# Three-layer decoder on one core: the mask of two pairs added by VectorE, with the setup and the order of work rearranged

## The reference, cut to what matters

```
layer 0: causal self-attention, 16 heads, then x @ W_proj
layer 1: q from x; k, v from ctx; scores = where(mask == 0, -1e9, q k^T / 4); softmax; @ wo
layer 2: unmasked self-attention + mixture of 8 experts (softmax gate, top 2, x @ W_experts[e] + b)
x = layernorm(x + layer(x))
```

## Time and profile before

| | |
|---|---|
| median of 3 runs | 925.97 us (924.67 to 928.93) |
| profiled execution, its own time | 927.58 us |
| its span | 925.8 us |
| mean granted TensorE clock | 0.991 of full speed |
| PE / VectorE / ScalarE / POOL busy | 873.3 / 773.5 / 588.9 / 424.6 us |
| chain of work that ended last | PE 79%, ScalarE 7%, VectorE 5% |

### The profile page before, as it was taken

One profiled execution on the slowest core, in us unless ns is written; L12 is line 12 of the kernel. 1 busy time (PEld: TensorE's weight loads), 2 busy tenths in 40 slices (PEclk: granted clock), 3 DMA queues, 4 the chain that ended last, 5 costly groups with the idle time before them and its releaser, 6 DMA issues.

```text
span 925.8 us, 28627 instructions
## 1 busy us (share of the span) xinstructions
PE 873.3 (94%) x9980; PEld 742.9 (80%) x9980; DVE 773.5 (84%) x3776; ACT 588.9 (64%) x1211; POOL 424.6 (46%) x586
## 2 busy tenths in 40 slices
PE   5798999999889999999999899999999999999995
PEld 3687888888777888888888778888888888888874
DVE  4699898888988888888887878888888888888885
ACT  3578887788777787878787644545554455555533
POOL 5588887888775453545455323222222222222201
PEclk8999999999999999999999999999999999999999
DMA  4656564547445353434444222222222222222200
GB/s 150 171 152 164 145 182 125 160 140 198 113 123 142 104 153 100 132 107 128 118 110 110 76 66 70 82 82 82 81 82 82 82 82 82 82 80 82 82 13 24
DMA packets 98164, 100.48 MB, mean 109 GB/s; under 512 B 10701, under 2 KB 90599, under 8 KB 98023
## 3 DMA queue, kind: packets, MB, share of 16 engines
q1 hardware_dynamic: 98023, 98.66, 38.8%
HBM read 18.14 MB, written 4.19 MB: 24 GB/s over the span
## 4 chain that ended last, share of the span: by engine, by line
PE 79%; ACT 7%; DVE 5%; issue 3%; DMA 2%; SPq 2%; POOL 1%; ACTq 0%; POOLq 0%; DVEq 0%
PE work L495 43%; PE work L639 10%; PE scores L616 8%; PE max_scores L592 7%; PE work L648 4%; PE scores L619 3%; ACT attn L799 2%; PE work L520 1%; SPq L448 1%; DVE max_scores L967 1%; ACT x_all L821 1%; PE work L657 1%; ACT k_parts L757 1%; DMA q_stack<-neg_max_t 1%; PE work L682 1%
## 5 line engine op out<-in xcount | busy, mean ns | idle before, releaser
L967 DVE CUSTOM_DVE_ANT_0 max_scores<-max_scores,mask_qk 128x128 f32<-128x128 f32 x1024 | 261.6, 324 | 40.2 <-PE max_scores L592 40.1
L799 ACT ACTIVATE attn<-scores 128x512 f32<-128x512 f32 x384 | 215.3, 596 | 61.8 <-PE scores L616 56.9
L616 PE MATMUL scores<-q_stack,k_stack 128*128 128x128 bf16 x1536 | 140.7, 221 | 17.8 <-DMA q_stack<-neg_max_t 11.9
L592 PE MATMUL max_scores<-k_stack,q_stack 126*128 126x128 bf16 x1536 | 148.7, 221 | 6.0 <-DVE neg_max L967 2.4
L967 DVE DVE_READ_ACCUMULATOR2_ANT neg_max<- 128x1 f32 x1024 | 143.8, 140 | 0.0
L1079 POOL TENSOR_TENSOR q_full<-q_full,q_parts 128x512 f32<-128x512 f32 x48 | 56.4, 1176 | 173.7 <-ACT q_parts L757 173.6
L616 PEld LDWEIGHTS scores<-q_stack,k_stack 128*128 128x128 bf16 x1536 | 96.1, 98 | 45.7 <-DMA q_stack<-neg_max_t 16.7
L1040 DVE SCALAR_TENSOR_TENSOR x_all<-work,combine,x_all 128x256 f32<-128x256 f32 x256 | 122.7, 479 | 8.3 <-PE work L495 3.1
L592 PEld LDWEIGHTS max_scores<-k_stack,q_stack 126*128 126x128 bf16 x1536 | 99.3, 98 | 34.4 <-issue 13.4
L495 PE MATMUL work<-split_hi,w_hi 128*128 128x256 f32 x384 | 115.4, 301 | 7.7 <-DVE split_lo L868 7.5
L495 PE MATMUL work<-w_hi,split_hi 128*128 128x256 f32 (+2 forms) x320 | 114.9, 359 | 0.0
(11 more groups left out here) (125 smaller groups left out, 2059.2 us busy)
## 6 DMA issues: line engine op xcount, KB each, us to landing
k_stack<-k_parts SPq DMA_DIRECT2D x288, 128.0 KB, 2.4
q_stack<-q_parts SPq DMA_DIRECT2D x288, 128.0 KB, 2.6
in_t<-in_xt SPq DMA_DIRECT2D x16, 256.0 KB, 3.1
x_all<-in_x SPq DMA_DIRECT2D x16, 256.0 KB, 3.3
in_t<-in_ct SPq DMA_DIRECT2D x16, 256.0 KB, 3.5
out<-x_all SPq DMA_DIRECT2D x16, 256.0 KB, 2.1
stage<-in_e SPq DMA_DIRECT2D x4, 512.0 KB, 5.0
stage<-in_qk SPq DMA_DIRECT2D x2, 512.0 KB, 4.0
```

The costliest lines, as they stand in the source:

```text
L592: mm = pe.matmul(dst[:, b, h2, :], head(QS, n, 2 * p + h2, b, ROWS), head(KS, n, 2 * p + h2, b, ROWS), start=(b + h2 == 0), stop=(b + h2 = ...
L616: mm = pe.matmul(dst[:, b, h2, :], head(KS, n, 2 * p + h2, b, rows), head(QS, n, 2 * p + h2, b, rows), start=(b + h2 == 0), stop=(b + h2 = ...
L799: act.activation(attn("exp", n, p)[:, :, :], SS[g % 2][:, :, :, :].rearrange("k b h q -> k (b h) q"), ACT.Exp).then_inc(probs_done, 1)
L967: ins = dve.tensor_tensor_reduce(scores, scores, MQ[l][:, :], -1.0, HUGE, ALU.add, ALU.min, NM[n % 2][:, b, h:h + 1])
```

## The change

1. `LIMITED = (2, 5)`: in the second layer's second pass, pairs 2 and 5 get no mask matmul on PE. A new piece `lim` on VectorE adds the mask in place in PSUM, and ScalarE's exponentials of these pairs wait for it.
2. `MAX_PE_ITEMS = 1`: for item 0 the causal mask is added by a PE matmul in pass one, and the maxima are one tensor_reduce per pair.
3. `K_ACT_ITEMS = 1`: item 0's k rows are issued by ScalarE's queue: part 0 behind k's high part, part 1 behind k's middle part, part 2 behind q's middle part.
4. Setup: the bias load has its own semaphore and q's scaled bias its own signal; the second low weights come ahead of the tables; POOL clears the third stack; POOL waits for `setup_v` only at item 0's residual.
5. New keys in `TIMES` and `PERIOD`, and `SHIFTS`, which moves kinds of items 0, 1, 15, 16, 31, 32, 46 and 47.

The diff, cut to its core:

```diff
+K_ACT_ITEMS = 1
+MAX_PE_ITEMS = 1
+LIMITED = (2, 5)
...
-PERIOD = [16.51, 18.09, 25.01]
+PERIOD = [16.52, 17.99, 25.0]
...
+SHIFTS = {
+    0: {"exp": -0.09, "in": -2.83, "k": 0.73, "ke": 0.65, "kh": 1.26, "kl": -0.38, "km": -0.38, ... "v": -2.94, "va": 1.39, "xl": 4.54, "zT": 0.43},
+    1: {"in": 6.26, "k": 0.7, "ke": 1.53, ... "v": -2.07, "va": -3.83, "xh": -5.85, "xl": -4.52, "z": 0.4, "zT": 1.27, "zh": -0.08, "zl": -0.02},
...
+def mask_in_max(n, p):
+    return n >= MAX_PE_ITEMS and layer(n) < 2 and p in MAX_DVE[layer(n)]
...
-ORDER = sorted([(base(n) + t, kind, n, part) for n in range(NITEM)
+ORDER = sorted([(base(n) + t + SHIFTS.get(n, {}).get(kind, 0.0), kind, n, part) for n in range(NITEM)
...
+        def stack_rows(queue, x, n, k):
+            if n < STACKS and k == 0:
+                queue.wait_ge(stacks_clear, n + 1)
...
             def k_stack(n, k):
-                stack_rows("k", n, k)
+                if n >= K_ACT_ITEMS:
+                    stack_rows(sp, "k", n, k)
...
             def scores(n, p):
-                l, g, rows = layer(n), S2_TURN[(n, p)], P
+                g, rows = S2_TURN[(n, p)], P
+                added = layer(n) == 1 and p not in LIMITED
...
-                if l == 1:
+                if added:
                     mm = pe.matmul(dst[:, :, :, :], IDB[:, :], MK[:, :].unsqueeze(1).to_broadcast([P, 2 * PB, P]),
                                    start=False, stop=True, skip_group_check=True)
...
-            act.wait_ge(setup_v, 1)
+            act.wait_ge(q_bias_done, 1)
...
             def k_high(n, part):
                 high("k", n)
+                if n < K_ACT_ITEMS:
+                    stack_rows(act, "k", n, 0)
 
             def q_middle(n, part):
                 middle("q", n)
+                if n < K_ACT_ITEMS:
+                    stack_rows(act, "k", n, 2)
 
             def k_middle(n, part):
                 middle("k", n)
+                if n < K_ACT_ITEMS:
+                    stack_rows(act, "k", n, 1)
...
             def probs(n, p):
                 g = S2_TURN[(n, p)]
-                act.wait_ge(score_psum, g + 1)
+                if layer(n) == 1 and p in LIMITED:
+                    act.wait_ge(limited, count("lim", n, LIMITED.index(p)))
+                else:
+                    act.wait_ge(score_psum, g + 1)
...
             x_low(0, 0)
+            dve.wait_ge(bias_loaded, 16)
+            dve.tensor_scalar(QBI[:, :, :], COLB[:, :, 0, :], SCALE, None, ALU.mult).then_inc(q_bias_done, 1)
+            first_low(1)
             dve.wait_ge(const_loaded, 16 * CONSTS)
-            setup_link(dve.tensor_scalar(QBI[:, :, :], COLB[:, :, 0, :], SCALE, None, ALU.mult))
...
             dve.memset(SPARE[:, :], 0.0).then_inc(setup_v, 1)
-            first_low(1)
-            dve.wait_ge(first_lo, 2)
-            dve.memset(pairs_of(QS[2]), 0.0)
-            dve.memset(pairs_of(KS[2]), TWO_ONES).then_inc(last_stack_clear, 1)
...
-                if l < 2 and p in MAX_DVE[l]:
+                if mask_in_max(n, p):
...
+            def limit(n, j):
+                g = S2_TURN[(n, LIMITED[j])]
+                dve.wait_ge(score_psum, g + 1)
+                scores = SS[g % 2][:, :, :, :].rearrange("k b h q -> k (b h) q")
+                dve.tensor_tensor(scores, scores, MK[:, :].unsqueeze(1).to_broadcast([P, 2 * PB, P]),
+                                  ALU.add).then_inc(limited, 1)
...
-            for j in range(2):
+            for j in range(STACKS):
+                if j == STACKS - 1:
+                    pool.wait_ge(first_lo, 1)
                 pool.memset(pairs_of(QS[j]), 0.0)
+                if j == STACKS - 1:
+                    pool.wait_ge(first_lo, 2)
                 pool.memset(pairs_of(KS[j]), TWO_ONES).then_inc(stacks_clear, 1)
-            pool.wait_ge(setup_v, 1)
...
+                if n == 0:
+                    pool.wait_ge(setup_v, 1)
```

More of the change, by code:

```diff
@@ L58 @@
 RB_COLS = 2 * D + E
[L62 removed]
+PERIOD = [16.52, 17.99, 25.0]
 TIMES = [
[4 rows of a table removed]
[L69 removed]
[4 rows of a table removed]
[L74 removed]
[4 rows of a table removed]
[L79 removed]
[9 rows of a table removed]
[L89 removed]
[3 rows of a table removed]
[L93 to L97 removed]
[4 rows of a table added]
+     "max": [-18.76, -17.7, -13.25, -11.85, -11.55, -9.49, -6.51, -4.89], "nm": [-3.71], "maxt": [-3.26],
[4 rows of a table added]
+     "norm": [31.45], "causal": [3.54, 3.95, 4.71, 5.28, 7.4, 8.24, 9.86, 10.35], "va": [-15.09]},
[4 rows of a table added]
+     "max": [-16.43, -14.98, -13.59, -12.09, -10.71, -8.85, -6.15, -6.12], "nm": [-5.86], "maxt": [-3.88],
[4 rows of a table added]
+     "sum": [22.8], "rs": [24.44], "norm": [32.29], "va": [-11.66], "lim": [4.43, 6.68]},
[4 rows of a table added]
+     "max": [-26.23, -24.29, -22.41, -19.38, -16.69, -15.48, -13.52, -10.83], "nm": [-6.52], "maxt": [-7.2],
[3 rows of a table added]
+     "gtop": [-19.94], "gateT": [-15.22], "cbt": [-15.78], "bias": [-14.42], "eb": [-14.29],
+     "expert": [-7.28, -6.62, -4.09, 1.07, 3.62, 5.54, 8.04, 13.62],
+     "combine": [-5.91, -4.51, -1.57, 1.69, 4.94, 6.01, 9.62, 15.3], "zadd": [13.69, 23.55], "stat": [24.6],
+     "rs": [28.58], "norm": [31.42], "store": [28.89]},
+]
+SHIFTS = {
[8 rows of a table added]
+}
 PIECES = ["qk1", "vo1", "qk2", "vg2", "e0", "e1", "e2", "e3"]
@@ L317, in decoder @@
         WB = [stack.enter_context(nc.psum_tensor(f"work{i}", [P, 512], F32)) for i in range(WORK_BANKS)]
-        const_loaded, setup_v, setup_p, dve_setup, stacks_clear, last_stack_clear = sem("const_loaded"), sem("setup_v"), sem("setup_p"), sem("dve_setup"), sem("stacks_clear"), sem("last_stack_clear")
+        const_loaded, bias_loaded, setup_v, setup_p, dve_setup, stacks_clear = (
+            sem(name) for name in ("const_loaded", "bias_loaded", "setup_v", "setup_p", "dve_setup", "stacks_clear"))
+        q_bias_done = sem("q_bias_done")
         first_loaded = [sem(f"first_loaded{j}") for j in range(2)]
@@ L408, in decoder @@
         MI, MF = MASKS[:, 0:2 * P].bitcast(mybir.dt.int32), MASKS[:, 2 * P:4 * P]
-        CONSTS = 5
+        CONSTS = 4
+        def stack_rows(queue, x, n, k):
+            if n < STACKS and k == 0:
+                queue.wait_ge(stacks_clear, n + 1)
+            if n >= STACKS and k == 0:
+                queue.wait_ge(score_psum, S2_TURN[(n - STACKS, PAIRS - 1)] + 1)
+            queue.wait_ge((hi_done, mid_done, low_done)[k][x], n + 1)
+            for j, part in enumerate(Q_PART if x == "q" else K_PART):
+                if part == k:
+                    queue.dma_start((QS if x == "q" else KS)[n % STACKS][j:P:STRIDE, :, :, :],
+                                 PART[x][:, k, :, :]).then_inc(stacked[(x, k)], 16)
         block = stack.enter_context(nc.Block())
@@ L435, in load_rows @@
                 sp.dma_start(pair(n), t["x"][n]).then_inc(x_loaded[n % 4], 16)
[L437 to L449 removed]
             def q_stack(n, k):
[L452 removed]
+                stack_rows(sp, "q", n, k)
             def k_stack(n, k):
[L455 removed]
+                if n >= K_ACT_ITEMS:
+                    stack_rows(sp, "k", n, k)
             def max_load(n, part):
@@ L482, in _ @@
             sp.wait_ge(const_loaded, 16 * CONSTS)
+            sp.wait_ge(bias_loaded, 16)
         @block.tensor
@@ L579, in max_scores @@
                 l, g = layer(n), S1_TURN[(n, p)]
-                added = l < 2 and p not in MAX_DVE[l]
+                added = l < 2 and not mask_in_max(n, p)
                 if n == 0 and p == 0:
@@ L616, in scores @@
                         mm = pe.matmul(dst[:, b, h2, :], head(KS, n, 2 * p + h2, b, rows), head(QS, n, 2 * p + h2, b, rows),
-                                       start=(b + h2 == 0), stop=(b + h2 == 2 and l != 1), skip_group_check=True)
-                if l == 1:
+                                       start=(b + h2 == 0), stop=(b + h2 == 2 and not added), skip_group_check=True)
+                if added:
                     mm = pe.matmul(dst[:, :, :, :], IDB[:, :], MK[:, :].unsqueeze(1).to_broadcast([P, 2 * PB, P]),
@@ L1060, in _ @@
             work = {"bor": bias_sum, "wlo": piece_low, "xl": x_low_later, "cl": c_low, "ve": v, "gtop": gate_top, "max": row_max,
-                    "nm": max_parts, "z": z_tokens, "zl": z_low, "sum": out_sum, "cbt": gate_t,
+                    "nm": max_parts, "lim": limit, "z": z_tokens, "zl": z_low, "sum": out_sum, "cbt": gate_t,
                     "eb": expert_bias, "combine": combine, "zadd": z_add, "stat": moe_statistics}
```

18 lines of the change are left out of this document (2 added, 16 removed), and 55 rows, old and new, of tables (SHIFTS, TIMES).

## The result

The changed kernel takes 929.05 us, the kernel before, run beside it, 926.39: 1.0033 times as long (95% interval 1.0021 to 1.0044). That is a small loss, inside the 0.5% that the forecast called "same", and 3.3 us over the forecast of 925.7.

A forecast was written before the change was run, and what follows sets the result against it. PE was taken to bound the second and third layers, PE and VectorE together the first. 5.0 - 3.0 - 1.5 - 0.8 = -0.3 us gave 927.3, or 925.7 on the median's scale; range 921 to 931, with rivals 915 to 935.

The forecast's parts named there:

- Part A: Second layer, masks of pairs 2 and 5 moved from PE to VectorE: +5.0 us, bounds +4.7 and +17.
- The loop of 16.20: Second layer: s1.7 waits for VectorE's max.5, so a steady step takes 16.20 us against 15.87; 12 steps, +4.0.
- the slow addition: Rival, second layer: an addition is as slow as PSUM-to-PSUM work, 0.99 us; +12, 938 us; chance 0.16.
- The step from item 16 to 17: Entry to the second layer: additions on a VectorE full from 286 us, only part hidden; +0.9 us.
- The steps to 30, 31 and 32: Into the third layer: -0.4 at item 30 for two saved matmuls, +0.5 at 31 and 32 for VectorE's gate work.
- exp.3 now behind k's copy: Second layer: this makes s2.5 some 0.3 us late, but the stall vanishes in PE's 0.7 us idle per item.
- Part B: Setup and item 0, start of the first layer: -3.0 us, bounds -5.5 and 0.
- Part C: First layer's order: s1.2 between s2.0 and s2.1, 0.22 us earlier on some 10 of 15 steps; -1.5, bounds -4 and +3.
- Part D: The tail: expert 7 and s2.7 go ahead of zT.0, so s2.7 gains 0.33 + 0.45; -0.8 us.
- PE as the bound: Rival, second layer: PE stays the bound, masks bring 16 x -0.44 = -7.0; sum -12.3, 914 us; chance 0.17.
- the lost early gain: Rival: VectorE is full in the first layer, Part B and Part C bring 0; sum +4.2, 930 us; chance 0.15.
- part C at its bound: Rival, first layer: the reordering is worth its bound of -4; sum -2.8, 923 us; chance 0.12.

The follow-up runs named there:

- a_nolim: The changed kernel with all eight second-pass masks of the second layer back on PE, no VectorE additions: 930.54 us, 1.0051 of the kernel before.
- a_l1b: The changed kernel with the second layer's keys, period and PE masks of the kernel before, no additions, no shifts of items 16 and 31: 926.40 us, 1.0004.
- a_kva_cl: The changed kernel, second layer: k's projection and ScalarE's k and v copies put back, context's low copy out of VectorE's loop: 923.89 once; 925.23, 0.9996 in 12 runs (a_kva_cl5).
- a_full_cl: The changed kernel with PE's and ScalarE's old second-layer order, additions kept, context's low copy out of VectorE's loop: 926.11 us, 1.0002 of the kernel before.
- b_lim: The kernel before, own order, setup and keys, with only the second layer's two VectorE mask additions put in: 939.43 us, step 16.44.
- b_setup: The changed kernel's setup code with all keys and periods of the kernel before, no shifts, no additions: 926.65 us.

## Why the prediction was right or wrong

The forecast had the changed kernel 0.3 us faster; it is 2.7 slower, so the sign was wrong too.

**Part A is the step that failed: it put the new order of PE and ScalarE in the second layer at nothing, and the steps behind the changes of layer at +0.9 and +0.1.** It said +5.0; from item 16 to item 32 the trace has +9.8 (-7.46 to +2.33). By its own steps:
- The price of an addition, 0.60 taken: 0.61 and 0.64. Right; the slow addition (0.99) is out.
- The loop of 16.20: 16.30, with PE waiting ahead of s1.7. A steady step costs 0.43 in place of 0.33: items 21 to 29 +3.45 for 2.6. PE is busy for 183.6 of 190 us, where 181 was forecast. The wait there is smaller than forecast (0.29 seen in the row, 0.7 forecast): PE is held elsewhere too, and its weight loads wait for ScalarE's copies and exponentials as well (2.2 and 2.0 us in the eight steps from 364 to 492).
- "The step from item 16 to 17 ...: +0.9" was the one exception allowed. Three of the next five steps, to items 17, 19 and 20, are long (17.90, 17.34, 17.49; the other two are 16.05 and 16.07), +4.65 in all, where the forecast had 2.2. a_nolim has them without additions (84.89 for the five, 84.85 after), a_l1b without the new order does not (80.49; 80.20 before). So the second layer's new keys are enough to cost them, without additions. With PE's and ScalarE's order put back and cl out it is still 82.31 (a_kva_cl) and 82.63 (a_full_cl), and the additions alone, in the old order, make it 83.60 (b_lim): what each piece costs there was not isolated.
- The steps to 30, 31 and 32, forecast at +0.1 together, took +1.69; the saving of 0.4 at item 30 did not come (18.64 for 18.65), and 1.10 came back at item 33. The cause of this loss stays open.
- Worst, the sentence that the stalls of "exp.3 now behind k's copy ... vanish in that idle time". In the steady step they do vanish behind VectorE's loop, but they are part of a second limit at 15.99, just under the first. Part A was priced as PE's masks against VectorE's additions; the new order stood at nothing, and costs 0.55 a step by itself (16.42 for 15.87), of which k's, ke's and va's places are 0.27. On top of it the additions *save* 0.12 (16.42 to 16.30), while in the old order they cost 0.57.

**Part B, -3.0**, was about right. The profiled pair says -4.05 at item 2. Executions scatter there: over sixteen profiled with the change's start, item 2 came from 62.47 to 65.05, mean 63.5; over three with the old start the mean is 67.0. So -3.5. PE's first work of item 1 came at 18.07 (forecast 18.4), maxt of item 0 at 34.40 (34.0), item 1's s1.0 at 36.14 (35.8), item 0's s2.0 at 37.58 (38.0), and ScalarE's issues took the 0.6 assumed:

```profile
13.65 1.91 ACTq L447 DMA_DIRECT2D k_stack<-k_parts  x3
```

The forecast had no clock in it. The kernel before loses some 1.5 us to the fall in item 1's step and the kernel after doesn't, so some two fifths of the gain are the clock's: the total is right in part by luck. b_setup has the change's setup code without its keys and is only 1.05 early at item 2, though it has no fall there either, so the code without its keys brings nothing by itself. The Trainium skill (DMA: Bandwidth & Descriptors, "Issuing engines are not separate DMA queues") calls the sequencer's time that issuing from several engines saves "usually small relative to the DMA itself". The trace shows 0.64 an issue; no run isolates what moving them to ScalarE saved.

**Part C, -1.5**, has the right sign, and its mechanism did not happen. VectorE's wait of 0.63 for s1.2 is still 0.60, and steps 3 to 7 are equal to 0.05. The gain of 3.4 sits in single steps: item 8 (17.09 to 15.56), 9, 14 and 16. Item 8's step has PE waits of 0.91 and 1.16 before, 0.36 and 0.38 after. b_setup, with the old keys, has 16.98 there, a_l1b, with the new ones, 15.57. But b_lim, with the old keys and no fall of the clock, has 15.94: the new keys themselves bring some 0.4, the absence of the fall the other 1.1. Which key it is, and what makes the gains at the other items, was not tried.

**Part D, -0.8**: -0.73. pv.1 waits 0.34 where it waited 0.78. **Third layer, 0**: steps of 23.72 for 23.77, right. The new line ran 96 masks on PE (L646) for 128, as forecast.

**The sum.** -3.5 - 3.4 + 9.8 - 1.1 - 0.2 - 0.7 = +0.9 against the forecast's -0.3. The measured medians differ by 2.7. Some 1.8 stay open. Falls of the clock in some executions and not in others would fit, since the times go with the granted clock: of the 20 executions after, the 11 at 0.993 have a median of 927.95 and the 9 at 0.991 one of 929.97, and the profiled one is of the faster group. Where in the kernel those falls lie is not shown. Of the rivals, PE as the bound, the slow addition and the lost early gain are refuted (the gain came and was spent); part C at its bound happened, under a larger part A. By the rule that the forecast took from the Trainium skill (VectorE: DVE Perf Modes, "The DRAIN you can't avoid"), that the next VectorE operation does not start until the pipe has emptied, an addition would cost an estimated 0.69, the page's 691 ns. The trace has 0.61 and 0.64, as a further sentence of that section allows: "A next op that is not held starts earlier".

No version beats the kernel before: a_kva_cl5, at 0.9996 of it, is the fastest (0.996 to 0.999 had been expected, a miss), 0.4% under the changed kernel (0.9996 / 1.0033), and its interval takes in 1.

## What to carry to other kernels

When an edit comes with a new order of work, price the order alone first: run, or work out, the new order without the edit. Here several limits lie within 0.6 us of each other (VectorE's loop, ScalarE's exponentials behind copies, PE's own work), so taking 0.44 from PE or 0.57 from VectorE gives back only what the next one allows. A lead won early is worth its size only if the seams between planned orders pass it on. And before a difference of 1 or 2 us is put down to an edit, compare the granted clock by stretches: two of the gains here are mostly a fall that one of the two profiled executions had.
